# Phase 1 of a spectral attention and mixture-of-experts kernel: second PSUM bank for turned rows, softmax without convolution taps between, value copies ahead of the exponentials

## What is computed

```
Xh = rfft(x in chunks of 64)                # 16 chunks per batch entry
low 4 frequencies  -> block-causal attention, 16 heads, 4 kv heads, real and imaginary part apart
high frequencies   -> depthwise causal convolution of 7 taps along frequency, gelu, 128x128 product, gate
x1 = layernorm(x + irfft(low and high joined))
logits of the experts = distances of x1 to 8 centroids
```

## Time and profile before

| | us |
|---|---|
| median of 3 runs (564.67 to 567.99) | 565.73 |
| the profiled execution | 564.46 |
| its span on the core, first to last instruction | 562.6 |
| phase 1, steps 3 to 7, one step | about 21.46 |

### The profile page before, as it was taken

How to read it: one execution, slowest core, us unless ns; L and a number is a source line. 1 busy time by engine, 2 the same in 40 slices (tenths; PEclk the granted TensorE clock), 3 DMA queues, 4 the chain that set the end, 5 groups by cost and what they waited for, 6 DMA issues and landing times.

```text
span 562.6 us, 13552 instructions
## 1 busy us (share of the span) xinstructions
PE 503.3 (89%) x3988; PEld 479.5 (85%) x3988; DVE 363.9 (65%) x1045; ACT 349.3 (62%) x744; POOL 293.3 (52%) x424
## 2 busy tenths in 40 slices
PE   4677988988989776899999999999999999999990
PEld 4575977977977665799999999999999999999980
DVE  3778798898898899534344465564646456666763
ACT  3565778888788565465555556666565656755651
POOL 0152544645635446454535455777776777754453
PEclk9979999999999965699999999999999999999996
DMA  8350264164153014100000001111111111100000
GB/s 226 121 129 10 69 157 126 53 164 130 50 158 91 2 46 52 24 22 22 16 22 17 21 17 31 31 40 31 40 30 42 34 37 35 34 20 16 20 30 28
DMA packets 47183, 31.56 MB, mean 56 GB/s; under 512 B 12123, under 2 KB 44710, under 8 KB 47126
## 3 DMA queue, kind: packets, MB, share of 16 engines
q1 hardware_dynamic: 42214, 21.77, 15.1%
q0 software_dynamic: 4096, 8.66, 5.6%
q10 hardware_dynamic: 816, 0.41, 0.3%
HBM read 22.13 MB, written 8.69 MB: 55 GB/s over the span
## 4 chain that ended last, share of the span: by engine, by line
PE 56%; DVE 4%; ACT 1%; issue 1%; POOL 0%; DVEq 0%; ACTq 0%
PE ps L1656 26%; PE ps L1681 18%; PE ps L1671 9%; PE ps L1665 1%; DVE xT L1310 1%; PE ps L1237 1%; POOL out_dram L1617 0%; ACT xT L1230 0%; DVE xs L1860 0%; DVEq L1586 0%; ACT L1764 0%; PE ps L1497 0%; DVE y L1827 0%; DVE ya L1823 0%; DVE yb L1825 0%
## 5 line engine op out<-in xcount | busy, mean ns | idle before, releaser
L1656 PE MATMUL ps<-wts,xh 128*128 x620 | 154.5, 333 | 0.0
L1847 DVE TENSOR_TENSOR h<-ps,sg 128x684 f32<-128x684 f32 x78 | 67.6, 866 | 90.0 <-PE ps L1656 82.3
L1634 POOL TENSOR_TENSOR xl<-xT,xh 127x128 fp32r<-127x128 f32 x155 | 68.0, 458 | 100.5 <-ACT xh L1750 100.4
L1681 PE MATMUL ps<-w2s,hT 115*128 (+1 forms) x930 | 116.6, 275 | 0.3 <-DVE xs L1860 0.3
L1681 PEld LDWEIGHTS ps<-w2s,hT 115*128 115x128 f32 (+1 forms) x930 | 110.0, 191 | 0.6 <-issue 0.6
L1656 PEld LDWEIGHTS ps<-wts,xh 128*128 128x128 f32 x620 | 104.8, 191 | 0.2
L1656 PE MATMUL ps<-wts,xl 128*128 x310 | 99.7, 321 | 0.0
L1764 ACT ACTIVATE sg<-ps 128x684 f32<-128x684 f32 x78 | 57.6, 739 | 66.2 <-PE ps L1656 66.2
L1773 ACT ACTIVATE hT<-ps 114x768 f32<-114x768 f32 x78 | 62.9, 806 | 55.9 <-PE ps L1671 55.9
L1860 DVE SCALAR_TENSOR_TENSOR xs<-ps,xs 128x128 f32 x155 | 54.4, 351 | 50.9 <-PE ps L1681 48.0
L1617 POOL DMA_INDIRECT out_dram<-xs,idx x64 | 62.8, 982 | 26.1 <-issue 17.6
(11 more groups left out here) (290 smaller groups left out, 840.9 us busy)
## 6 DMA issues: line engine op xcount, KB each, us to landing
xt<-_attn_hidden_states_dram SPq DMA_DIRECT2D x8, 512.0 KB, 6.1
xres<-_attn_hidden_states_dram SPq DMA_DIRECT2D x7, 512.0 KB, 5.2
rows_dram<-x1s SPq DMA_DIRECT2D x7, 512.0 KB, 3.7
w2s<-in_L_ffn_W_dram SPq DMA_DIRECT2D x8, 171.0 KB
st<-in_L_ffn_Wg_dram SPq DMA_DIRECT2D x8, 171.0 KB, 2.3
st<-in_L_ffn_W_dram SPq DMA_DIRECT2D x8, 171.0 KB, 2.4
stl<-in_L_ffn_Wg_dram SPq DMA_DIRECT2D x8, 171.0 KB, 3.3
stl<-in_L_ffn_W_dram SPq DMA_DIRECT2D x8, 171.0 KB, 4.0
```

The costliest lines, as they stand in the source:

```text
L1634: v.tensor_tensor(xl[0:D - 1, i % 2, u, :], xT[0:D - 1, bass.ds(off[u], P)], xh[0:D - 1, i % 2, u, :].bitcast(F32), ALU.subtract).then_inc ...
L1656: mm = pe.matmul(ps[:, 2 * w + u, 0:HF], a[:, t % 2, u, :], wflat[:, bass.ds(w1[u] + (b + w * HF), HF)], start=(k == 0), stop=(k == 2))
L1681: mm = pe.matmul(ps[:, low(t) + u, 0:D], hT[0:n, t % 2, u, k, :], w2flat[0:n, bass.ds(w1[2 + u] + k * D, D)], start=(k == 0), stop=(k == 2))
L1847: v.tensor_tensor(h[:, t % 2, 0:units(t), :], ps[:, 2:2 + units(t), 0:HF], sg[:, 0:units(t), :], ALU.mult).then_inc(s["h_done"], 1)
```

## The change

The change touches the step of phase 1 in four places, all in the written order or in the choice of a bank.

1. `turned(1)` writes bank 0 in place of bank 7, so it no longer waits for ACT's copy of the first half out of bank 7. The centroid product L557 waits for the first half of x1T ahead of its first four products and for the second ahead of the last four, in place of both at once.
2. ACT: Vs half 0, exponential half 0, Vs half 1, exponential half 1, then both x1T copies. Before: exponential 0, x1T 0, Vs 0 and 1, x1T 1, exponential 1.
3. DVE: taps 2, 3 and 4 of the imaginary convolution no longer stand between the score and sum instructions. They follow the residual sum.
4. So the residual sum xres directly follows the reciprocals with nothing between any of the softmax instructions.

The tail is the same in both.

```diff
@@ PE @@
                 def turned(h):
-                    pe.wait_ge(s["x1t_ev"], 2 * (t - 2) + h)
                     for j in range(4):
-                        mm = pe.transpose(ps[:, 7, j * P:(j + 1) * P], x1s[:, 4 * h + j, :], ident)
+                        mm = pe.transpose(ps[:, (7, 0)[h], j * P:(j + 1) * P], x1s[:, 4 * h + j, :], ident)
...
-                    pe.wait_ge(s["x1t_ev"], 2 * (t - 1))
                     for j in range(TB):
+                        if j % 4 == 0:
+                            pe.wait_ge(s["x1t_ev"], 2 * (t - 2) + j // 4 + 1)
                         mm = pe.matmul(ps[:, 7, j * C:(j + 1) * C], x1T[:, j, :], cT[:, :], start=True, stop=True)
@@ ACT @@
-                if X:
-                    softmax(0)
-                if T:
-                    turned(0)
-                if Y:
-                    for h in range(2):
+                for h in range(2):
+                    if Y:
                         act.wait_ge(s["vt_done"], 2 * (t - 1) + h + 1)
...
+                    if X:
+                        softmax(h)
                 if T:
+                    turned(0)
                     turned(1)
-                if X:
-                    softmax(1)
@@ DVE @@
                     scores(0)
-                    conv(t, 1, not Y, range(2, 3))
                     scores(1)
-                    conv(t, 1, not Y, range(3, 4))
...
-                        if i == 0:
-                            conv(t, 1, not Y, range(4, 5))
...
-                    conv(t, 1, not Y, range(5, KS))
+                    conv(t, 1, not Y, range(2, KS))
```

More of the change, by code:

```diff
@@ L668, in turned @@
                     act.wait_ge(s["r_done"], t - 2)
-                    nc.scalar.activation(x1T[:, 4 * h:4 * h + 4, :].rearrange("p j m -> p (j m)"), ps[:, 7, :], ACT.Copy).then_inc(s["x1t_ev"], 1)
+                    nc.scalar.activation(x1T[:, 4 * h:4 * h + 4, :].rearrange("p j m -> p (j m)"), ps[:, (7, 0)[h], :], ACT.Copy).then_inc(s["x1t_ev"], 1)
                 def gelu(b, i, first):
```

## The result

The changed kernel took 569.71 us (median of 8 executions, 567.46 to 570.77) against 565.2 us for the kernel before (8 executions, 563.93 to 567.99). The recorded ratio is 1.0053, with a 95% interval of 1.0033 to 1.0073; it is an estimate of its own and not the quotient of the two medians, which is 1.0080. The changed kernel is slower by half a percent. The interval leaves out 1, and the ratio lies right at the half percent (1.005) that the prediction takes as the least that can be told from none. The profiled execution of it, 567.46 us with a span of 565.6, was the shortest of its runs. Against the profiled execution of before (564.46, span 562.6) that is +3.0 us.

The account below looks back on a forecast made before the run. PE leads, with DVE and ACT nearly full; PE plus 1.69 us of idle sets the step. 3.4 + 0.3 - 0.7 + 0.3 = +3.3, rounded to +3.0, on the median 565.73 gives 568.7 us, range 565.0 to 571.3.

Parts of the forecast that it names:

- The removed wait wins nothing: PE ahead of the second four turns: 1.32 us of idle go, their worth decided by ACT, which gives DVE nothing.
- The exposed load eats the gain on ACT: ACT: about 1.1 us saved by displaced x1T copies is spent on the exposed table load; exponential 1 at 159.04 against 158.93.
- The taps use up the cover ahead of XL: DVE behind xres: three taps add 2.0 us against about 1.1 us of slack; L475 at 167.5 against 166.85.
- The step, 22.14 us: Phase 1 loop through softmax, taps, statistics and XL: 22.14 us against 21.46, +0.68 a step.
- The second loop (rival 2): Loop through the load of xres: 21.91 us; rival: landing 5.5 us or later, +0.9 to +1.0 a passage, 570 to 571, chance 0.12.
- The five passages: Phase 1, step 2 to 3 up to 6 to 7: 5 x 0.68 = 3.4 us, bounds 2.0 to 6.5.
- Step 1 to 2, −0.7: Phase 1 without turns: xres at 51.5 against 52.25, XL's 2.42 us idle hides the taps; -0.7, bounds -2.4 and +1.0.
- Step 0 to 1, +0.3: Phase 1 start: taps now run beside both POOL products Pb; +0.3 us, bounds -0.2 to +0.8.
- Tail, +0.3: Tail: ACT's gelu at 162.1 in place of 160.90, so PT and PE work behind it come 0.3 us later.
- Rival 1: Taps hidden by 1.7 us of cover behind xres, removed wait shows: 564.1, or 562.4 without the slow-clock stretch; chance 0.12.
- Rival 3: Phase 1 loop: PE's idle grows, clock falls to 0.50 in some steps, 1.7 us each, 572 and more; chance 0.05.
- Rival 4: ACT: table load costs nothing where it is, exponential 1 1.3 us earlier, second loop bounds: +0.45 a passage, 567.5; chance 0.06.

Follow-up runs that it names:

- the repeat: The changed kernel, unchanged, measured once more against the kernel before: 568.07 us, ratio 1.0034.
- Bank 0 alone: The kernel before with only the second four turned rows in bank 0 and the centroid product's wait split: 565.73 us, ratio 1.0004.
- taps alone: The kernel before with only its three taps moved behind xres: 569.34 us, ratio 1.0067.
- taps put back: The changed kernel with its three taps back among the softmax instructions, bank 0 and ACT's new order kept: 566.32 us, ratio 1.0014.
- The early table load: The changed kernel with a one-column exponential of a spare tile ahead of the first Vs copy: 566.94 us; with xres loaded first also, 561.11 us.
- load-first kernel: The changed kernel with SyncE issuing the load of xres ahead of the store of x1s: 569.38 us, ratio 1.0069.
- early load with taps put back: The changed kernel with three taps back among the softmax instructions and a spare-tile exponential ahead of the first Vs copy: 569.39 us, ratio 1.0074.

## Why the prediction was right, point by point

Forecast and measurement agree in sign, size and cause: 568.7 forecast, 569.71 and in the repeat 568.07 measured. Between the profiled executions +3.0 was forecast and +3.0 found, and that exact hit is luck: the terms found are +3.54 - 1.64 + 0.22 + 0.08 in phase 1, and +0.8 in phase 2, for which the sum had no term. Single terms were off, and cancelled.

- **The removed wait wins nothing.** Right. Bank 0 alone measured 1.0004, and the idle stands ahead of the Vs products.
- **The exposed load eats the gain on ACT.** Right: exponential 1 at 4.06 us, forecast 4.24, before 4.13. The load ends at 137.45 and the exponential starts at 137.46. The drain of about 1380 ns that the Trainium skill names (ScalarE: Activation LUTs, "What ACT_TABLE_LOAD costs") does not show here.
- **The taps use up the cover ahead of XL.** Right, and shown from both sides: taps alone 1.0067, taps put back 1.0014. XL starts 11.79 us behind the first turns, forecast 12.1, and PE waits 0.66 us for it, forecast 0.9.
- **The step, 22.14 us.** This term of the sum was too long: 21.88 undisturbed, +0.43 a step and not +0.68; the prediction's lower bound was +0.4. The measured hand-overs give the loop again: 9.50 + 1.13 + 0.62 + 1.29 + 0.54 + 0.48 + 0.65 + 0.93 + 1.20 + 3.39 + 1.56 + 0.59 = 21.88. The difference lies in exponential 0 to Vs 1 (0.54, not 0.66), the delay of XL by POOL (0, not 0.1), statistics to XL (1.56, not 1.65) and crumbs. I had added whole durations where neighbours on an engine overlap by up to a tenth. On POOL, L1042 (L1049 before) runs from 144.76 to 146.40, 0.19 us into XL, and XL took 0.54 in place of 0.49.
- **The second loop (rival 2).** Real, and the prediction took too little of it into the sum. The five passages cost 110.69 less 107.15 = +3.54 us, forecast 3.4; of that five times 0.43 is 2.15, and most of the rest belongs to the step that waited 0.97 us for xres. So this term came out right with its two parts, the loop and the wait, off in opposite directions. In the repeat, with one wait of 0.2 us, they took 109.44: +2.29. The early table load with and without the load first (1.0028 and 0.9914) shows this loop directly.
- **Step 1 to 2, −0.7.** −1.64 in the first profile and about +0.2 in the repeat. The fault was to give the half-clock stretch no chance of its own in the sum: it comes and goes between executions, and at 1.9 us it is larger than the term. Where it is absent, XL binds already in step 2 (the 0.64 us at 58.19), which the prediction had taken as hidden.
- **Step 0 to 1, +0.3.** VT of step 1 came at 46.45 against 46.23: +0.22.
- **Tail, +0.3.** From the last first turns to phase 2 the time grew by 0.08 (29.51 to 29.59). What is left of the span's 3.0 us, 0.8, lies in phase 2, which the change doesn't touch. Why it is longer there wasn't traced.
- **Rivals 1, 3 and 4.** Rival 1 (taps hidden) fell: PE waits for XL in every step. Rival 3 (clock in the loop) is in neither profiled execution; see the open point. Rival 4 (a load that costs nothing where it stands) fell: it is seen in ACT's row, and taking it away together with the late load won 0.8 us a step.

Open: some medians lie 2 to 4 us above the profiled execution of the same kernel (the changed kernel 2.2, the load-first kernel 3.2, the taps alone 4.2). The mean granted clock goes with it in two of the three. Of the kernel with the taps alone, the five executions with a mean of 0.951 to 0.956 took 565.19 to 567.18 us and the seven with 0.945 took 569.17 to 571.35, and the load-first kernel divides the same way. In the first set of the changed kernel it does not: two executions at 0.957 took 569.83 and 570.67 us, as long as those at 0.944 and 0.945. The profiles of the load-first kernel and of the taps alone are of executions with the higher clock, so what the loop costs is read from their steps and not from their medians, and rival 3 isn't ruled out for the longer executions. The slow stretch in step 2 and the landing of xres give a part of the spread. The rest was not traced.

## What to carry to other kernels

Before a wait is removed, follow the work behind it to its next wait, and before work is moved into a gap-free stretch, look up how long its first consumer's engine can still wait: here 1.1 us of cover met 2.0 us of moved work, and 1.3 us of removed idle met another wait on the same engine. Loops through an engine and through a transfer can lie close together, here within about 0.2 us: write down the length of each, and relieve them together, as early table load and load first did (together −0.9%; of the two alone, neither was faster than the kernel before). Put movable work where its engine idles (two taps away from the stretch behind xres, one of them to where DVE waited for the scores: 0.9914 to 0.9813).

## What the runs showed of the hardware

- **Two transfers on one queue.** With the store first, the load of xres landed in 5.4 us and the store in 3.7; with the load first it was 4.0 and 5.3. Being second costs the load 1.4 us and the store 1.6. The groups of DMA issues on the page of the changed kernel (KB each, median us to landing):

```profile
xres<-_attn_hidden_states_dram SPq DMA_DIRECT2D x7, 512.0 KB, 5.4
rows_dram<-x1s SPq DMA_DIRECT2D x7, 512.0 KB, 3.7
```

and of the one with the load first:

```profile
xres<-_attn_hidden_states_dram SPq DMA_DIRECT2D x7, 512.0 KB, 4.0
rows_dram<-x1s SPq DMA_DIRECT2D x7, 512.0 KB, 5.3
```

- **Taps beside POOL.** In step 0 of the changed kernel POOL's products of L1037 run from 26.96 for 2.39 us, and DVE's five taps beside them take 4.11 us, against 3.23 in the later steps:

```profile
26.96 2.39 POOL L1037 TENSOR_TENSOR Pb<-Sb,rs 128x512 f32<-128x512 f32 x2 [8.86 <-DVE rs L920]
27.59 4.11 DVE L831 SCALAR_TENSOR_TENSOR YI<-XF,dw,YI 128x416 f32<-128x416 f32 x5
```

The Trainium skill (SBUF — State Buffer, "SBUF: two separate sides") names such an operation, with two inputs in SBUF, as one that POOL can block while it reads SBUF. The 0.88 us agree with it in direction; that a tap waits for the whole of POOL's instruction is not shown.

- **The clock.** The same idle of PE can be followed by full or by half clock: 1.56 us ahead of L454 in two executions of one program (1.00 and 0.50), and 0.34 + 0.95 us in each step of the early load with taps put back, where the clock fell in two of five steps.
